# Two copies a unit earlier, and three PSUM banks for turned weights in a soft mixture of experts

## The chip, the cores and the metric

The kernel runs on one core of a Trainium2 chip. The metric is the device time of one execution in microseconds (us); the median of several executions counts. The engines are TensorE (PE: matrix products and transposes; PEld: its weight loads), VectorE (DVE), ScalarE (ACT), GpSimd (POOL) and SyncE (SP, which here only issues transfers). Each works through its own instructions in order, and they are held together by semaphores. PSUM, into which TensorE writes, has eight banks of 128 x 512 float32.

## The reference, cut to what matters

A block of three residual stages on x, 4 x 256 tokens of 256 channels: a cross attention over 4096 context rows, a causal self attention with 16 heads, and a soft mixture of 64 experts with 32 slots each. The change lies in the last one:

```python
h = layernorm(x)                                            # 1024 tokens x 256
logits = einsum('tzd,ed->tze', h, phi_w) + phi_b            # 1024 x 2048
D = softmax(logits, over the 32 slots of an expert)         # "dispatch"
C = softmax(logits, over the 64 experts of a slot)          # "combine"
X = clip(einsum('tznp,tzd->npd', D, h), -33000, 65000)      # 2048 slots x 256
X = tanh((X - mean) * rsqrt(var + 1e-5))
Y = einsum('npd,ndH->npH', X, expert_w) + expert_b          # 64 experts
y = einsum('tznp,npH->tzH', C, Y)                           # 1024 x 256
out = x + y
```

## The kernel before, in words

The 1024 tokens are 8 tiles of 128 (`TT`). The 2048 slots are cut in two ways: into 4 blocks of 512 columns for the logits (`LB`), so that there are 32 units of one tile and one block (`NU`, unit u is tile u // 4, block u % 4), and into 16 steps of 128 slots or 4 experts (`ST`) for the experts. Every engine has its own program, written out by hand as loops; the order of the work is the order of the calls in them.

*Logits stage.* For each unit, TensorE makes the logits in one of four banks (`logit`, L1774), ScalarE brings them out (`logits_out`, L1908), VectorE takes the maximum of each expert's slots (`dispatch_max`, L2007) and subtracts it straight from the bank (`dispatch_subtract`, L2012; for every fourth unit GpSimd does so from SBUF, L1724), ScalarE takes exponentials (`dispatch_exp`, L1913), VectorE sums and inverts (L2019, L2024), and GpSimd multiplies (`divide_dispatch`, L1697). TensorE starts unit u only when the bank of unit u - 4 is free (`evicted`). From unit 5 on each unit is followed by slot inputs (`early_inputs`, L1781): products of the divided dispatch weights with the normed rows `h_nat`, summed in banks 4 to 7. Beside it ScalarE takes the combine exponentials of tiles 0 to 3 by slot, four per unit from its eighth round on (`slot_exp`, L1919), from the maxima over a whole tile that VectorE takes in its rounds 4, 11, 18, 25, 28 and 31 (`combine_max`, L2028). Behind the 32 units come the remaining slot inputs (L1781, L1787).

The last two tiles of x are finished only when this stage begins. So VectorE norms tiles 6 and 7 (`norm`, L1994) in its round 2. TensorE turns the normed rows of tiles 4 to 7 behind the logits of unit 4 (`transpose_h`, L1766) into banks 6 and 7 (`PS_TURN`). In their round 5 (`v == LB + 1`) VectorE (L2051) and ScalarE (L1943) copy them to `hT`, which shows as `turned`. TensorE waits for both copies behind the logits of unit 7, since the slot inputs of slots 512 on write the same banks. Unit 16 is the first to read the copies.

*Experts stage.* VectorE clips the slot inputs and takes their statistics (`input_statistics`), GpSimd the scale, ScalarE the tanh (`input_tanh`, L1961). In step s TensorE turns the inputs of step s (`transpose_inputs`, L1805, two transposes) into bank 4 or 5, ScalarE copies them out (L1975), and TensorE multiplies the inputs of step s - 1 with their weights (`experts`, L1815, 16 instructions). VectorE adds the bias (`outputs`, L2079), ScalarE and GpSimd split the sum into a high and a low part (L1933, L1752), and `mix` adds three products of each step to the result of a tile (L1823, L1825, L1826).

For `mix` the combine weights have to be turned as well. A turn (`transpose_combine`, L1797) is four transposes into one bank, bank 0 or 1 in turns; ScalarE casts it to the high part (`combine_out`, L1929), VectorE takes the low part as bank minus high part (`combine_low`, L2085), and then the bank is free. A tile has four turns. Tiles 0 to 3 are turned in steps 4 to 7, two turns ahead of the step's experts and two behind; tiles 4 and 5 in steps 12 to 15, two turns in each; tiles 6 and 7 after the steps. ScalarE's order in a step is: tanh of the next step, copy of the turned inputs, the casts, high part of an output of two steps before. The expert weights (1 MB a step) come in through three buffers, each transfer waiting for the products of the step that used the buffer.

Of the kernel before, what the change touches and what calls it, by code (L numbers as in the profile page):

```python
# [45 lines left out]
def at_least(eng, sem, value):  # L46

    if not isinstance(value, int) or value > 0:
        eng.wait_ge(sem, value)
# [1481 lines left out]
def soft_moe(nc, x_sb, x_stats, x_mv, x_ve, x_rstd, ident, kept, disp, highs, y_hi, y_lo, expert_w, expert_b, out):  # L1531
# [18 lines left out]
    with ExitStack() as st:  # L1550
# [39 lines left out]
                   front_hi[:, 1, :]]  # L1590

        bank = kept.bank
        psL, psT, psE, psC = bank[0:4], bank[4:6], bank[6:8], bank[0:2]
        psY = [bank[2 + t // 2][:, t % 2 * HID:(t % 2 + 1) * HID] for t in range(TT // 2)] + [
            bank[t][:, 0:HID] for t in range(TT // 2, TT)]
        Y_FROM = (6, 7, 8, 9)
# [54 lines left out]
        def turned_at(s):  # L1651

            if 4 <= s < 8:
                return s - 4, 0, LB
            return (s // 2 - 2, s % 2 * 2, s % 2 * 2 + 2) if 12 <= s else None

        def mixed_until(t, s):

# [103 lines left out]
        def _(pe):  # L1762
# [29 lines left out]
            def transpose_combine(c, first, end):  # L1792
                for k in range(first, end):
                    pe.wait_ge(cmul_g, LB * c + k + 1)
                    at_least(pe, cTlo_v, LB * c + k - 1)
                    for j in range(4):
                        last = nc.tensor.transpose(psC[k % 2][:, j * P:(j + 1) * P],  # L1797
                                                   comb[:, c, (4 * k + j) * P:(4 * k + j + 1) * P], ident[:])
                    last.then_inc(cT_mm, 1)

            def transpose_inputs(s):
                pe.wait_ge(tanh_a, s + 1)
                at_least(pe, xT_a, s - 1)
                for c in range(DH):
                    last = nc.tensor.transpose(psT[s % 2][:, c * P:(c + 1) * P], xh[:, s % 2, c * P:(c + 1) * P], ident[:])  # L1805
                last.then_inc(xT_mm, 1)

            def experts(s):
# [49 lines left out]
            slot_inputs(EARLY + 4, 0, TT)  # L1858
            slot_inputs(EARLY + 5, 0, TT)
            for s in range(ST):  # L1860
                if s < 2:
                    pe.wait_ge(clip_v, 2 * s + 2)
                transpose_inputs(s)
                turn = turned_at(s)
                if s == 4:
                    pe.wait_ge(clip_v, EARLY + 4)
                if turn is not None:
                    transpose_combine(turn[0], turn[1], turn[1] + 2)
                if 1 <= s <= 2:
                    pe.wait_ge(clip_v, 2 * s + 4)  # L1870
                if s:
                    experts(s - 1)
                if s < 2:
                    slot_inputs(EARLY + 6 + s, 0, TT)
                for t in range(TT // 2):
                    first, end = mixed_until(t, s - 1), mixed_until(t, s)
                    if first == 0 and end > 0:
                        pe.wait_ge(clip_v, 14 if t < 2 else ST)
                        pe.wait_ge(cTlo_v, LB * (t + 1))
                    if end > first:  # L1880
                        mix(t, first, end)
                    if t == 0 and turn is not None and turn[2] > turn[1] + 2:
                        transpose_combine(turn[0], turn[1] + 2, turn[2])
# [19 lines left out]
        @block.scalar  # L1903
        def _(act):
            def logits_out(u):
                t, cols = unit(u)
                act.wait_ge(L_mm, u + 1)
                nc.scalar.copy(comb[:, t, cols], psL[u % 4][:]).then_inc(L_a, 1)  # L1908

            def dispatch_exp(u):  # L1910
                t, cols = unit(u)
                subtracted(act, u)
                nc.scalar.activation(disp[t][:, cols], disp[t][:, cols], ACT.Exp).then_inc(dexp_a, 1)  # L1913

            def slot_exp(i):
                c, p = i // NS, i % NS
                act.wait_ge(cneg_v, c + 1)
                column = by_slot(comb[:, c, :])[:, p, :]
                nc.scalar.activation(column, column, ACT.Exp, bias=cneg[:, c, p:p + 1],  # L1919
                                     accum_out=csum[:, c, p:p + 1]).then_inc(cslot_a, 1)  # L1920

            def combine_exp(c):
                act.wait_ge(csub_g, LB * (c - SLOTWISE + 1))
                nc.scalar.activation(comb[:, c, :], comb[:, c, :], ACT.Exp).then_inc(cexp_a, 1)

            def combine_out(c, first, end):
                for k in range(first, end):
                    act.wait_ge(cT_mm, LB * c + k + 1)
                    nc.scalar.copy(comb_hi[c][:, k * 512:(k + 1) * 512], psC[k % 2][:]).then_inc(cT_a, 1)  # L1929

            def outputs_high(s):
                act.wait_ge(mixed_v, s + 1)
                nc.scalar.copy(y_hi[:, s, :], mixed[:, s, :]).then_inc(yhi_a, 1)  # L1933

            logits_out(0)
            logits_out(1)
            slot = 0
            for v in range(NU + 1):
                if v:
                    dispatch_exp(v - 1)  # L1940
                if v == LB + 1:
                    act.wait_ge(pro_mm, 2)
                    nc.scalar.copy(hT[:, 1, HALF:2 * HALF], PS_TURN[1][:]).then_inc(pro_a, 1)  # L1943
                if v + 2 < NU:
                    logits_out(v + 2)
                if v >= FIRST_SLOTS:
                    for _ in range(PER_STEP):
                        slot_exp(slot)
                        slot += 1

            def input_tanh(s):
                q = s // 2
                if s % 2 == 0:
                    act.wait_ge(srstd_g, q + 1)
                    nc.scalar.activation(sneg[:, q, :], srstd[:, q, :], ACT.Identity, scale=-1.0).then_inc(shift_a, 1)
                    act.wait_ge(shift_a, 3 * q + 1)
                    for k in (0, 1):
                        nc.scalar.activation(snmr[:, q, k:k + 1], smv[:, q, k, 0:1], ACT.Identity, scale=sneg[:, q, k:k + 1]).then_inc(shift_a, 1)
                act.wait_ge(shift_a, 3 * q + 2 + s % 2)
                at_least(act, xT_mm, s - 1)  # L1960
                nc.scalar.activation(xh[:, s % 2, :], centred(s), ACT.Tanh, bias=snmr[:, q, s % 2:s % 2 + 1],  # L1961
                                     scale=srstd[:, q, s % 2:s % 2 + 1]).then_inc(tanh_a, 1)

            while slot < SLOTWISE * NS:
                slot_exp(slot)
                slot += 1
            combine_exp(SLOTWISE)
            combine_exp(SLOTWISE + 1)
            input_tanh(0)
            for s in range(ST):  # L1970
                if s + 1 < ST:
                    input_tanh(s + 1)
                act.wait_ge(xT_mm, s + 1)
                at_least(act, e_mm, s - 1)
                nc.scalar.copy(xhT[:, s % 2, :, :].rearrange("p c s -> p (c s)"), psT[s % 2][:, 0:DH * P]).then_inc(xT_a, 1)  # L1975
                if turned_at(s) is not None:
                    combine_out(*turned_at(s))
                if s == 2:
                    act.wait_ge(xs_mm, ST)
                if s >= 2:  # L1980
                    outputs_high(s - 2)
                if s in (8, 10):
                    combine_exp(SLOTWISE + s // 2 - 2)
            outputs_high(ST - 2)
            outputs_high(ST - 1)
            combine_out(TT - 2, 0, LB)
            act.wait_ge(ylo_g, ST)
            combine_out(TT - 1, 0, LB)

        @block.vector  # L1990
        def _(dve):
# [48 lines left out]
            for v in range(NU + 1):  # L2040
                if v < NU and not on_pool(v):
                    dispatch_subtract(v)
                if v + 1 < NU:
                    dispatch_max(v + 1)
                if v == 2:
                    dve.wait_ge(rstd_g, 2)
                    norm(TT - QT, TT)
                if v == LB + 1:
                    dve.wait_ge(pro_mm, 1)
                    dve.wait_ge(pro_v, 1)  # L2050
                    nc.vector.tensor_scalar(hT[:, 0, HALF:2 * HALF], PS_TURN[0][:], rest_rows[:], ident[:, 0:1],  # L2051
                                            ALU.mult, ALU.add).then_inc(pro_v, 1)
# [28 lines left out]
            def combine_low(c, first, end):  # L2081
                for k in range(first, end):
                    cols = slice(k * 512, (k + 1) * 512)
                    dve.wait_ge(cT_a, LB * c + k + 1)
                    nc.vector.tensor_tensor(comb_lo[:, c, cols], psC[k % 2][:], comb_hi[c][:, cols].bitcast(F32),  # L2085
                                            ALU.subtract).then_inc(cTlo_v, 1)

            combine_max(TT - 2)
# [87 lines left out]
```

## Time and profile before

| | us |
|---|---|
| median of 3 runs | 567.41 |
| the runs | 563.71, 567.92, 567.41 |
| profiled execution | 567.7 |
| its span, first to last instruction | 565.9 |
| TensorE busy | 533.9 (94%) |
| VectorE busy | 363.3 (64%) |
| ScalarE busy | 363.8 (64%) |
| GpSimd busy | 361.7 (64%) |

Mean granted TensorE clock 0.991 of full speed. The logits stage begins at 357.4 us of the span. Times of rows are counted from the start of the span. A row of a timeline gives the start, the duration, the engine, the line of the kernel, the operation, what it writes and reads, and how many instructions are merged in it; in brackets stands how long the engine was idle before, and what ended that. A merged row ends with the last instruction's end; TensorE's next instruction can start some 0.16 us before that, since its ends are modelled.

### The profile page before, as it was taken

What the parts mean: (1) busy time and instruction counts of PE and PEld (TensorE: products, weight loads), DVE (VectorE), ACT (ScalarE), POOL (GpSimd) and SP (SyncE); (2) the same over time, 40 slices, a digit from 0 to 9 for tenths busy, and PEclk for the clock granted to TensorE, in tenths of its full rate; (3) what the DMA queues carried; (4) which work ended last, traced back from release to release, by engine and by line L of the source; (5) the groups of instructions that cost most, each with busy time, mean ns of one, the idle gap of its engine ahead of it and who ended that gap; (6) DMA issues with size and microseconds to landing.
All of it is one profiled execution on the core that took longest, in us unless ns stands there. A gap on an engine that the chain in (4) does not pass through costs nothing. (4 is left out here: it accounts for less than half of the span.)

```text
span 565.9 us, 9355 instructions
## 1 busy us (share of the span) xinstructions
PE 533.9 (94%) x3256; PEld 414.5 (73%) x3256; DVE 363.3 (64%) x736; ACT 363.8 (64%) x1016; POOL 361.7 (64%) x282
## 2 busy tenths in 40 slices
PE   5898999999999999999898989889999999899998
PEld 4786888888888888777566656446555887578898
DVE  1785344564455345745776898686999998588340
ACT  2446765856584866873787886328999895666320
POOL 2775989659775784755559675243465899688500
PEclk9999999999999999999898999999999999999999
DMA  8463464675743733175139500400000643978110
GB/s 295 160 224 134 163 224 162 185 282 183 251 149 131 248 143 103 48 169 136 32 100 204 181 1 1 151 0 1 1 1 1 118 105 109 331 230 245 57 48 28
DMA packets 38669, 75.45 MB, mean 133 GB/s; under 512 B 3408, under 2 KB 27360, under 8 KB 37728
## 3 DMA queue, kind: packets, MB, share of 16 engines
q1 hardware_dynamic: 36864, 68.57, 39.6%
q10 hardware_dynamic: 1760, 6.30, 3.1%
q8 instruction: 26, 0.43, 0.3%
q14 instruction: 19, 0.16, 0.1%
HBM read 68.56 MB, written 6.30 MB: 132 GB/s over the span
## 5 line engine op out<-in xcount | busy, mean ns | idle before, releaser
L387 POOL TENSOR_TENSOR ctxT_lo<-front,ctxT_hi 128x1024 fp32r<-128x1024 f32 x32 | 76.9, 2408 | 46.2 <-ACT ctxT_hi L682 46.2
L503 PE MATMUL ps<-ctx_both,pT_hi 128*128 128x512 f32 x256 | 94.6, 409 | 1.9 <-DVE pT_lo L858 1.9
L392 POOL TENSOR_TENSOR ctx_both<-ctx_in,ctx_both 128x1024 fp32r<-128x1024 f32 x32 | 76.5, 2395 | 16.3 <-ACT ctx_both L687 16.3
L505 PE MATMUL ps<-ctx_both,pT_lo 128*128 128x256 f32 x256 | 71.9, 281 | 0.0
L1774 PE MATMUL ps<-front,turned 128*128 128x512 f32 x128 | 61.0, 605 | 0.3 <-PEq L1008 0.3
L850 DVE TENSOR_SCALAR_CACHE_REDUCE first<-ps,qbk 128x512 f32<-128x512 f32 x32 | 24.0, 750 | 55.5 <-PE ps L475 53.2
L706 ACT CAST pT_hi<-ps 128x512 fp32r<-128x512 f32 x64 | 34.0, 590 | 38.3 <-PE ps L487 38.3
L503 PEld LDWEIGHTS ps<-ctx_both,pT_hi 128*128 128x128 f32 x256 | 48.2, 188 | 13.1 <-DVE pT_lo L858 2.8
L858 DVE TENSOR_TENSOR pT_lo<-ps,pT_hi 128x512 fp32r<-128x512 f32 x64 | 41.1, 685 | 16.4 <-ACT pT_hi L706 16.4
L1919 ACT ACTIVATE comb<-comb,cneg 128x64 f32<-128x64 f32 x128 | 50.8, 411 | 0.0
L505 PEld LDWEIGHTS ps<-ctx_both,pT_lo 128*128 128x128 f32 x256 | 48.5, 190 | 0.1
L475 PE MATMUL ps<-ctxT_hi,qk_hi 128*128 128x512 f32 x128 | 41.1, 402 | 2.6 <-DVE qk_lo L842 2.2
L1710 POOL TENSOR_TENSOR comb<-comb,cinv 128x512 f32<-128x512 f32 x32 | 40.6, 1285 | 0.8 <-DVE cinv L2037 0.8
L475 PE MATMUL ps<-ctxT_hi,qk_lo 128*128 128x512 f32 x128 | 40.0, 394 | 0.0
L475 PE MATMUL ps<-ctxT_lo,qk_hi 128*128 128x512 f32 x128 | 39.7, 391 | 0.0
L682 ACT CAST ctxT_hi<-front 128x1024 fp32r<-128x1024 f32 x32 | 33.7, 1057 | 8.1 <-PE ps L475 3.8
L1774 PEld LDWEIGHTS ps<-front,turned 128*128 128x128 f32 x128 | 24.4, 193 | 19.7 <-issue 18.2
L1697 POOL TENSOR_TENSOR more<-more,dinv 128x512 f32<-128x512 f32 x24 | 25.1, 1048 | 19.6 <-DVE dinv L2024 19.6
L1409 DVE TENSOR_REDUCE nmax<-ps 128x2 f32<-128x512 f32 (+1 forms) x48 | 31.6, 671 | 7.9 <-PE ps L1210 6.9
L1826 PE MATMUL ps<-y_hi,comb_lo 128*128 128x256 f32 x128 | 36.1, 282 | 0.0
L1105 POOL TENSOR_TENSOR eB<-eB,rinv 128x1024 f32<-128x1024 f32 x16 | 30.3, 1893 | 8.9 <-DVE rinv L1417 8.9
L1351 ACT ACTIVATE eB<-ps,nmax 128x256 f32<-128x256 f32 x64 | 29.8, 483 | 8.9 <-DVE nmax L1409 8.9
(260 smaller groups left out, 1436.1 us busy)
## 6 DMA issues: line engine op xcount, KB each, us to landing
front<-in_ctx_turned_dram SPq DMA_DIRECT2D x32, 512.0 KB, 4.7
ctx_in<-in_ctx_dram SPq DMA_DIRECT2D x32, 512.0 KB, 3.5
back<-in_L_ffn_expert_w_dram SPq DMA_DIRECT2D x11, 1024.0 KB, 5.9
turned<-in_L_ffn_expert_w_dram SPq DMA_DIRECT2D x5, 1024.0 KB, 5.8
phi_piece<-in_phi_turned_dram ACTq DMA_DIRECT2D x8, 512.0 KB, 6.3
phi_less_dram<-phi_piece ACTq DMA_DIRECT2D x4, 512.0 KB, 3.1
front<-phi_less_dram SPq DMA_DIRECT2D x1, 2048.0 KB, 14.0
front<-in_L_ffn_expert_b_dram SPq DMA_DIRECT2D x4, 512.0 KB, 10.2
```

The source lines that it names most:

```text
L387: nc.gpsimd.tensor_tensor(ctxT_lo[:, n % RING, :, :], turned_in[:, n % SLOTS, :, :], ctxT_hi[:, n % RING, :, :].bitcast(F32), ALU.subtract ...
L392: nc.gpsimd.tensor_tensor(ctx_both[:, m % RING, :, 1, :], by_tile(m), ctx_both[:, m % RING, :, 0, :].bitcast(F32), ALU.subtract).then_inc( ...
L475: last = nc.tensor.matmul(pS[q][:], a[:, dh, q * P:(q + 1) * P], k[:, n % RING, dh, :], start=step == 0, stop=step == 5)
L503: nc.tensor.matmul(pO[q][:], pT_hi[:, c % 2, q, cols], ctx_both[:, m % RING, j, :, :].rearrange("p k d -> p (k d)"), start=c == 0 and j == ...
L505: last = nc.tensor.matmul(pO[q][:, 0:D], pT_lo[:, c % 2, q, cols], ctx_both[:, m % RING, j, 0, :], start=False, stop=c == NCH - 1 and j == ...
L682: nc.scalar.copy(ctxT_hi[:, n % RING, :, :], turned_in[:, n % SLOTS, :, :]).then_inc(ctxThi_a, 1)
L706: nc.scalar.copy(pT_hi[:, c % 2, q, :], probs_banks(c)[q][:]).then_inc(probsThi_a, 1)
L858: nc.vector.tensor_tensor(pT_lo[:, c % 2, q, :], probs_banks(c)[q][:], pT_hi[:, c % 2, q, :].bitcast(F32), ALU.subtract).then_inc(probsTlo ...
L1710: nc.gpsimd.tensor_tensor(part, part, cinv[:, c, :].unsqueeze(1).broadcast_to([P, EB, NS]), ALU.mult).then_inc(cmul_g, 1)
L1774: last = nc.tensor.matmul(psL[u % 4][:], hT[:, c, t * P:(t + 1) * P], phiT[:, c, cols], start=c == 0, stop=c == DH - 1)
L1826: last = nc.tensor.matmul(psY[t], comb_lo[:, t, cols], y_hi[:, s, :], start=False, stop=s == ST - 1, skip_group_check=True)
L1919: nc.scalar.activation(column, column, ACT.Exp, bias=cneg[:, c, p:p + 1], accum_out=csum[:, c, p:p + 1]).then_inc(cslot_a, 1)
```

## The change

The kernel does the same arithmetic. In the logits stage VectorE norms tiles 6 and 7 in its round 1 instead of 2, and VectorE and ScalarE copy the turned rows in round 4 instead of 5 (on VectorE ahead of that round's sum and of the tile maximum, on ScalarE ahead of bringing out unit 6). In the experts stage the turned inputs always go to bank 4, and the turned weights of tiles 0 to 5 go round banks 0, 1 and 5; those of tiles 6 and 7 keep banks 0 and 1. The waits follow: a turn waits for the low part three turns back instead of two, and the inputs' transposes of step s for the copy of step s - 1 instead of s - 2.

```diff
                    front_hi[:, 1, :]]
 
         bank = kept.bank
-        psL, psT, psE, psC = bank[0:4], bank[4:6], bank[6:8], bank[0:2]
+        psL, psT, psE, psC = bank[0:4], bank[4], bank[6:8], (bank[0], bank[1], bank[5])
         psY = [bank[2 + t // 2][:, t % 2 * HID:(t % 2 + 1) * HID] for t in range(TT // 2)] + [
             bank[t][:, 0:HID] for t in range(TT // 2, TT)]
         Y_FROM = (6, 7, 8, 9)
@@ -1653,6 +1653,10 @@
             if 4 <= s < 8:
                 return s - 4, 0, LB
             return (s // 2 - 2, s % 2 * 2, s % 2 * 2 + 2) if 12 <= s else None
+
+        def turn_bank(c, k):
+
+            return psC[(LB * c + k) % 3 if c < TT - 2 else k % 2]
 
         def mixed_until(t, s):
 
@@ -1792,17 +1796,17 @@
             def transpose_combine(c, first, end):
                 for k in range(first, end):
                     pe.wait_ge(cmul_g, LB * c + k + 1)
-                    at_least(pe, cTlo_v, LB * c + k - 1)
+                    at_least(pe, cTlo_v, LB * c + k - (2 if c < TT - 2 else 1))
                     for j in range(4):
-                        last = nc.tensor.transpose(psC[k % 2][:, j * P:(j + 1) * P],
+                        last = nc.tensor.transpose(turn_bank(c, k)[:, j * P:(j + 1) * P],
                                                    comb[:, c, (4 * k + j) * P:(4 * k + j + 1) * P], ident[:])
                     last.then_inc(cT_mm, 1)
 
             def transpose_inputs(s):
                 pe.wait_ge(tanh_a, s + 1)
-                at_least(pe, xT_a, s - 1)
+                at_least(pe, xT_a, s)
                 for c in range(DH):
-                    last = nc.tensor.transpose(psT[s % 2][:, c * P:(c + 1) * P], xh[:, s % 2, c * P:(c + 1) * P], ident[:])
+                    last = nc.tensor.transpose(psT[:, c * P:(c + 1) * P], xh[:, s % 2, c * P:(c + 1) * P], ident[:])
                 last.then_inc(xT_mm, 1)
 
             def experts(s):
@@ -1858,8 +1862,8 @@
             slot_inputs(EARLY + 4, 0, TT)
             slot_inputs(EARLY + 5, 0, TT)
             for s in range(ST):
-                if s < 2:
-                    pe.wait_ge(clip_v, 2 * s + 2)
+                if s == 0:
+                    pe.wait_ge(clip_v, 2)
                 transpose_inputs(s)
                 turn = turned_at(s)
                 if s == 4:
@@ -1926,7 +1930,7 @@
             def combine_out(c, first, end):
                 for k in range(first, end):
                     act.wait_ge(cT_mm, LB * c + k + 1)
-                    nc.scalar.copy(comb_hi[c][:, k * 512:(k + 1) * 512], psC[k % 2][:]).then_inc(cT_a, 1)
+                    nc.scalar.copy(comb_hi[c][:, k * 512:(k + 1) * 512], turn_bank(c, k)[:]).then_inc(cT_a, 1)
 
             def outputs_high(s):
                 act.wait_ge(mixed_v, s + 1)
@@ -1938,7 +1942,7 @@
             for v in range(NU + 1):
                 if v:
                     dispatch_exp(v - 1)
-                if v == LB + 1:
+                if v == LB:
                     act.wait_ge(pro_mm, 2)
                     nc.scalar.copy(hT[:, 1, HALF:2 * HALF], PS_TURN[1][:]).then_inc(pro_a, 1)
                 if v + 2 < NU:
@@ -1972,7 +1976,7 @@
                     input_tanh(s + 1)
                 act.wait_ge(xT_mm, s + 1)
                 at_least(act, e_mm, s - 1)
-                nc.scalar.copy(xhT[:, s % 2, :, :].rearrange("p c s -> p (c s)"), psT[s % 2][:, 0:DH * P]).then_inc(xT_a, 1)
+                nc.scalar.copy(xhT[:, s % 2, :, :].rearrange("p c s -> p (c s)"), psT[:, 0:DH * P]).then_inc(xT_a, 1)
                 if turned_at(s) is not None:
                     combine_out(*turned_at(s))
                 if s == 2:
@@ -2042,10 +2046,10 @@
                     dispatch_subtract(v)
                 if v + 1 < NU:
                     dispatch_max(v + 1)
-                if v == 2:
+                if v == 1:
                     dve.wait_ge(rstd_g, 2)
                     norm(TT - QT, TT)
-                if v == LB + 1:
+                if v == LB:
                     dve.wait_ge(pro_mm, 1)
                     dve.wait_ge(pro_v, 1)
                     nc.vector.tensor_scalar(hT[:, 0, HALF:2 * HALF], PS_TURN[0][:], rest_rows[:], ident[:, 0:1],
@@ -2082,7 +2086,7 @@
                 for k in range(first, end):
                     cols = slice(k * 512, (k + 1) * 512)
                     dve.wait_ge(cT_a, LB * c + k + 1)
-                    nc.vector.tensor_tensor(comb_lo[:, c, cols], psC[k % 2][:], comb_hi[c][:, cols].bitcast(F32),
+                    nc.vector.tensor_tensor(comb_lo[:, c, cols], turn_bank(c, k)[:], comb_hi[c][:, cols].bitcast(F32),
                                             ALU.subtract).then_inc(cTlo_v, 1)
 
             combine_max(TT - 2)
```

## Rows read from the trace of the kernel before

**Rows 1.** Busy time by stretch: stretch, its length, engines' busy us, clock, DMA share, GB/s.

```profile
383.00:440.00 57.00, 57.00 (x179) 33.60 (x178) 50.25 (x82) 54.08 (x211) 30.74 (x29) 1.00 0.00 1
440.00:480.00 40.00, 40.00 (x222) 32.69 (x221) 38.40 (x82) 31.67 (x120) 36.19 (x35) 1.00 0.49 109
480.00:500.00 20.00, 17.28 (x167) 12.39 (x169) 12.55 (x23) 13.99 (x34) 13.05 (x15) 1.00 0.92 288
500.00:566.00 66.00, 62.40 (x579) 55.26 (x571) 32.96 (x41) 23.42 (x51) 29.57 (x28) 1.00 0.37 119
```

**Rows 2.** Timeline of TensorE, start of the logits stage.

```profile
357.41 8.82 PE L1774 MATMUL ps<-front,turned 128*128 128x512 f32 x20 [0.32 <-PEq L1008]
...
367.58 1.09 PE L1766 MATMUL ps<-ident,wide 128*128 128x128 f32 x8 [1.35 <-DVE wide L1994]
368.51 1.88 PE L1774 MATMUL ps<-front,turned 128*128 128x512 f32 x4
...
373.67 1.88 PE L1774 MATMUL ps<-front,turned 128*128 128x512 f32 x4
378.11 1.13 PE L1781 MATMUL ps<-wide,first 128*128 128x256 f32 x4 [2.55 <-DVE turned L2051]
379.07 3.29 PE L1774 MATMUL ps<-front,turned 128*128 128x512 f32 x4
...
383.35 1.88 PE L1774 MATMUL ps<-front,turned 128*128 128x512 f32 x4
```

**Rows 3.** One microsecond of the same table by stretches.

```profile
381.00:382.00 1.00, 1.00 (x2) 0.34 (x1) 0.00 (x0) 0.00 (x0) 1.00 (x2) 0.50 0.00 0
```

**Rows 4.** Timeline of VectorE, the same stretch.

```profile
363.45 0.69 DVE L2007 TENSOR_REDUCE dmax<-comb 128x16 f32<-128x512 f32 x1 [0.30 <-ACT comb L1908]
...
366.07 1.46 DVE L1994 TENSOR_SCALAR wide<-x_sb,x_mv,x_rstd 128x256 f32<-128x256 f32 x2
...
372.53 3.61 DVE L2028 TENSOR_REDUCE cneg<-comb 128x32 f32<-128x2048 f32 x1
376.05 0.69 DVE L2012 TENSOR_TENSOR first<-ps,dmax 128x512 f32<-128x512 f32 x1
...
377.24 0.81 DVE L2051 TENSOR_SCALAR turned<-ps,rest_rows,ident 128x512 f32<-128x512 f32 x1
```

**Rows 5.** Timeline of GpSimd, the same stretch.

```profile
366.23 1.15 POOL L1724 TENSOR_TENSOR first<-comb,dmax 128x512 f32<-128x512 f32 x1
...
379.01 1.05 POOL L1697 TENSOR_TENSOR first<-first,dinv 128x512 f32<-128x512 f32 x1 [5.27 <-DVE dinv L2024]
```

**Rows 6.** Waits from 480 to 500 us: total us, times, longest.

```profile
PE ps L1797 <- DVE comb_lo L2085: 2.7, 4, 0.8
```

**Rows 7.** The table by stretches, 376 to 396 us.

```profile
376.00:396.00 20.00, 17.89 (x51) 10.51 (x52) 13.57 (x27) 12.65 (x45) 8.34 (x8) 0.91 0.00 1
```

**Rows 8.** Timeline of TensorE in the experts stage.

```profile
479.11 0.44 PE L1805 MATMUL ps<-ident,xh 128*128 128x128 f32 x2
479.39 1.04 PE L1797 MATMUL ps<-ident,comb 128*128 128x128 f32 x8
...
481.48 1.23 PE L1797 MATMUL ps<-ident,comb 128*128 128x128 f32 x8
...
483.60 1.23 PE L1797 MATMUL ps<-ident,comb 128*128 128x128 f32 x8 [0.67 <-DVE comb_lo L2085]
...
522.75 1.22 PE L1797 MATMUL ps<-ident,comb 128*128 128x128 f32 x8
```

**Rows 9.** Timeline of ScalarE in the experts stage.

```profile
478.50 0.35 ACT L1975 COPY xhT<-ps 128x256 f32<-128x256 f32 x1
...
482.14 1.19 ACT L1929 CAST first_hi<-ps 128x512 fp32r<-128x512 f32 x2 [1.05 <-PE ps L1797]
...
484.90 1.06 ACT L1929 CAST first_hi<-ps 128x512 fp32r<-128x512 f32 x2
```

**Rows 10.** Timeline of VectorE in the experts stage.

```profile
485.52 1.29 DVE L2085 TENSOR_TENSOR comb_lo<-ps,first_hi 128x512 fp32r<-128x512 f32 x2 [1.46 <-ACT first_hi L1929]
```

## The prediction

> **What bounds the kernel now.** I read the table by stretches first. From 383 to 480 us TensorE is busy for the whole of both stretches, while VectorE has 50.25 and ScalarE 54.08 of the first 57 us: there TensorE sets the pace, with ScalarE close behind. From 480 to 500 it is busy for 17.28 of 20 us, so something else ends steps there; after 500 it has 62.40 of 66 [rows 1]. What is shifted ahead of 383 us arrives at the end if the others can follow; what is saved between 480 and 500 arrives too.
>
> Then TensorE's timeline at the start of the logits stage. Twenty matmul instructions (units 0 to 4, four each, 0.43 us apart) start at 357.41, so unit 5 could follow at 366.01. The eight transposes of the last tiles' normed rows start at 367.58, released by VectorE's norm. Units 5 and 7 start at 368.51 and 373.67: 2.58 us per unit (1.72 for the logits, 0.86 for the slot inputs that follow). Unit 7's logits leave TensorE free at 373.67 + 1.72 = 375.39, but the slot inputs start at 378.11, released by VectorE's copy of the turned rows. The logits of unit 8 then take 3.29 us instead of 1.88, and unit 9 starts only at 383.35 [rows 2]. The reader is to see three losses in one place. The third is the clock: the granted clock was 0.50 (the 1.2 GHz level) at 381 us, after TensorE had stood still from 375.4 to 378.1, and 1.00 (2.4 GHz) from 383 on [rows 1, 3].
>
> VectorE's timeline says why. The norm runs at 366.07, after the third unit's work. The copy of the turned rows runs at 377.24, behind a 3.61 us maximum over a whole tile (372.53) and behind the next unit's subtraction (376.05) [rows 4]. Its input was there since the transposes ended, near 368.7.
>
> **Part one, the logits.** Nothing is added or removed; two norms and two copies go one unit earlier on their engines.
>
> *The norm.* It would follow the maximum at 363.45, so from 364.05. It took 1.46 us where it stood, while GpSimd ran an operation of 1.15 us from 366.23 [rows 4, 5]; I let it take as long at 364. It is done by 365.5 and TensorE no longer waits at 366.01. Gain: 367.58 - 366.01 = 1.57, and no less than the 1.35 that the trace marks as idle; I take 1.5. Behind the norm on VectorE stand sum and reciprocal of unit 0 and the subtraction of unit 2, which with it move back by its length, to an end near 366.9. Unit 6's logits overwrite that bank; they start near 369.5 (366.0 for the transposes, 0.93 for these, 2.58 for unit 5). This cover is 2.6 us; if it were gone, unit 6 would be late by the difference. Ahead of 369.7 us VectorE has done the same work in both orders.
>
> *The copies.* Unit 5's logits end near 368.7, ScalarE brings them out by 369.4, VectorE takes their maximum by 370.9 and then copies the turned rows: 0.81 us, done near 371.7 [rows 4]. ScalarE's copy goes ahead of bringing out unit 6, which is not there before 371: cost nothing, cover over 0.5 us. TensorE wants both copies after unit 7's logits, near 373.9, so the wait falls away whole: 378.11 - 375.39 = 2.72. The maximum over a tile comes 0.8 us later in its queue at most, ending at 376.1 as before; the subtraction of unit 5 ends by 376.7. TensorE wants its bank back for unit 9 near 377.3. That wait is late next, with 0.6 us to spare. After it comes GpSimd's division of unit 4, which started at 379.01 on VectorE's reciprocal [rows 5]. With the copy out of the way it starts near 378.2 and ends near 379.2, while TensorE asks for it at 379.0: between 0 and 0.3 us are paid. I take 0.1.
>
> *The clock.* From 378.11 to 383.35 TensorE did 3.44 us of work (0.86 + 1.72 + 0.86) in 5.24: 1.80 us lost [rows 2]. Without the two pauses it should not fall there. A gain of 0 to 1.8; I take 1.8, since between 480 and 500, with four marked pauses of 2.7 us in all, the longest 0.8, the granted clock stayed at 1.00 [rows 1, 6].
>
> Sum: 1.5 + 2.7 - 0.1 + 1.8 = 5.9.
>
> *Can the others follow?* The tile maximum that ends at 376.1 does not move, so VectorE must make up 5.9 us behind it. From 376 to 396 it was busy 13.57 of 20 us [rows 7]; that is 6.4 us idle, and 0.8 of copy is gone from there: 7.2 against 5.9. ScalarE was idle for more (12.65 busy). From 396 on every engine is in the state it was in, 5.9 us earlier, and TensorE stays the pace.
>
> **Part two, the experts.** Turn n (four transposes of a weight tile) needed VectorE's low part of turn n - 2, and now of turn n - 3, for tiles 0 to 5. The round trip: cast at 482.14, next turn at 483.60 after 0.67 us of waiting; 1.46 us from cast to release [rows 8, 9]. In steps 4 to 7 the marked pauses are 2.7 us [rows 6], and a group of eight transposes takes 1.23 us where its second turn waits, 1.04 where it does not [rows 8], which happens six times: 1.1 more. So 3.8 us can be had. Not all goes. ScalarE casts turns 2 and 3 from 482.14, and then has y_hi, the scale and shift, a tanh and the copy of the turned inputs before its next cast at 484.90; that one's low part starts at 485.52 [rows 9, 10]. Turn 7 now needs this low part (turn 4's), which ends near 486.2, while TensorE would be ready at 485.4. Going through the sixteen turns so, waits remain at turn 5 (0.5), 7 (0.8), 13 (0.4), 15 (0.3): 2.0. Gain 1.8. The group of eight at 522.75 (1.22 us) gives some 0.2 more [rows 8]. Sum 2.0; between 0 and 3.8.
>
> *The added wait.* The inputs' transposes of step s now wait for ScalarE's copy of step s - 1. Behind them on TensorE stand the turns and the experts' products, and through these VectorE's outputs. The tightest place is step 4: copy 478.50 to 478.85, transposes at 479.11 [rows 8, 9]; 0.26 us to spare. In the later steps the products and sums of a step of 4 to 5 us lie between. Cost nothing; if the cover at step 4 is gone, some tenths once. The dropped wait of step 1 was for work long done.
>
> The Trainium skill speaks against part two: its page "TensorE: Matmul & The Clock Gate", section "HAM oscillation — how this bites in real kernels", tells of a kernel in which "Adding PSUM double-buffering gave no further gain". By that the second part is worth 0 and the sum 5.9. No run here shows it yet; in the rows, VectorE's release of a bank ends the pauses.
>
> **Sum.** 5.9 + 2.0 = 7.9 us. The profiled execution took 567.7 us around its span of 565.9, the median of the runs is 567.4; 567.4 - 7.9 = 559.5.
>
> **The rivals.**
> *A, the forecast:* 559.5. Chance 0.56. Its own bounds: the gain lies between 5.4 + 0.5 and 6.1 + 3.8, so 557.5 to 561.5.
> *B, the third bank gives nothing,* because the chain cast, low part, turn stays as it is, or because the weight transfers bind (DMA share 0.92 from 480 to 500 [rows 1]): gain 5.9, time 561.5. Against it: the pauses end with VectorE's low part, not with a transfer. 0.16.
> *C, the clock falls all the same* in the logits' first units: 7.9 - 1.8 = 6.1, time 561.3. For it: TensorE's rate fell a microsecond after the pause had ended, so it may be decided by what lies before. 0.12.
> *D, VectorE becomes the bound after unit 8:* 7.2 us of slack is an average, and it may lie in the wrong places; then some 3 of the 5.9 are given back and the time is 562.5. 0.08.
> *E, slower:* with the experts' stage 6 us earlier and its pauses reshaped, the granted clock falls between 480 and 500. TensorE's work there is 17.28 us at full rate [rows 1]; each microsecond of it at half rate costs another. From 7.9 us of work at half rate on, the change loses; with all of it, 9.4 us are lost and the time is 576.8. Against it: 1.00 in that stretch, though it has the most pauses. 0.04. The same page of the Trainium skill, section "A second HAM failure mode: psum-queue depth-cycling", has a kernel that cycles through PSUM banks and whose clock goes up and down for it; here the trace shows the cycling (480 to 500) without the fall.
> The remaining 0.04: more than forecast, or a difference between executions.
>
> **How the numbers follow.** A measurement of this kernel tells about 1% (5.7 us) from no change, so faster means below 561.7. A lies there whole (0.56), B and C just inside with some two thirds of their chance (0.18), and 0.02 of the rest: 0.76. Slower: E, and a little for what I don't see, 0.05. Within 1%: 0.19. The range goes from A's lower bound, 557.5, to D's 562.5, with 0.8 added on both sides since one of the three runs lay 3.7 below the median: 556.7 to 563.3. Outside it are E and the odd differences, under 0.1 together, and of the rest what I have judged too narrowly.
>
> **What would show it.** Right: transposes at about 366.0 without a pause before them; no pause after unit 7; clock 1.00 from 366 to 386; unit 9 near 377.4; the last slot inputs ending 5.9 us earlier than before; TensorE's pauses before the turns between 475 and 495 down from 2.7 to below 2. Wrong: a new pause before unit 9 or 10 (released by VectorE or GpSimd), a pause before the inputs' transposes released by ScalarE's copy, VectorE without idle time after 390, or a granted clock below 1.00 at either place.

## The result and the profile after

The changed kernel took 558.21 us as the median of 4 runs (557.25 to 562.01), the kernel before 565.83 (563.71 to 567.92, now 4 runs). The ratio is 0.9858, with a 95% interval from 0.981 to 0.9906. A second series of the same kernel, in the experiments below, gave 0.9841 (0.9802 to 0.988). The forecast was 559.5, with a range from 556.7 to 563.3.

The head of the profile after, its line of busy times and the row of TensorE's granted clock in 40 slices:

```profile
span 556.0 us, 9354 instructions
...
PE 529.2 (95%) x3256; PEld 413.1 (74%) x3256; DVE 362.0 (65%) x736; ACT 363.4 (65%) x1016; POOL 361.6 (65%) x282
...
PEclk9999999999999999999899999999999999999999
```

The span is 556.0 us, 9.9 less than before, but not all of that is the change. The logits stage begins at 356.18 us instead of 357.41, and nothing ahead of it was touched. So every length below is counted from that stage's first matmul instruction: to the end it is 565.9 - 357.41 = 208.5 us before, and 556.0 - 356.18 = 199.8 after. The change is worth 8.7 us in these two profiles.

TensorE's timeline after, to be read against [rows 2] (times from the start of the span, duration, instruction, how many are merged, in brackets the idle time before):

```profile
356.18 8.82 PE L1778 MATMUL ps<-front,turned 128*128 128x512 f32 x20 [0.32 <-PEq L1008]
364.84 1.04 PE L1770 MATMUL ps<-ident,wide 128*128 128x128 f32 x8
365.71 1.88 PE L1778 MATMUL ps<-front,turned 128*128 128x512 f32 x4
367.43 1.03 PE L1785 MATMUL ps<-wide,first 128*128 128x256 f32 x4
368.29 1.88 PE L1778 MATMUL ps<-front,turned 128*128 128x512 f32 x4
370.01 1.03 PE L1785 MATMUL ps<-wide,first 128*128 128x256 f32 x4
370.87 1.88 PE L1778 MATMUL ps<-front,turned 128*128 128x512 f32 x4
372.59 1.03 PE L1785 MATMUL ps<-wide,first 128*128 128x256 f32 x4
373.45 1.88 PE L1778 MATMUL ps<-front,turned 128*128 128x512 f32 x4
...
376.03 1.88 PE L1778 MATMUL ps<-front,turned 128*128 128x512 f32 x4
```

The rows left out are of the same two kinds and have no bracket either. The reader is to see that none but the first has one. The transposes follow the twentieth logits instruction, the slot inputs at 372.59 follow unit 7, and unit 9 starts 376.03 - 356.18 = 19.85 us into the stage; before, it was 383.35 - 357.41 = 25.94 [rows 2]. That is 6.1 us.

VectorE's timeline after, for [rows 4]:

```profile
362.82 0.73 DVE L1998 TENSOR_SCALAR wide<-x_sb,x_mv,x_rstd 128x256 f32<-128x256 f32 x2
...
368.92 0.80 DVE L2055 TENSOR_SCALAR turned<-ps,rest_rows,ident 128x512 f32<-128x512 f32 x1
...
370.52 3.63 DVE L2032 TENSOR_REDUCE cneg<-comb 128x32 f32<-128x2048 f32 x1
374.08 0.68 DVE L2016 TENSOR_TENSOR first<-ps,dmax 128x512 f32<-128x512 f32 x1
```

The norm takes 0.73 us here instead of 1.46. The copy of the turned rows stands ahead of the tile maximum (370.52). The subtraction behind that is over at 374.76, and unit 9 wants its bank at 376.03.

The table by stretches after, for [rows 1, 3, 7], with the clock as the third number from the right, and TensorE's waits for the low part from 455 to 500 us, for [rows 6]:

```profile
374.00:382.00 8.00, 8.00 (x26) 4.63 (x25) 7.86 (x17) 5.85 (x19) 4.40 (x5) 1.00 0.00 0
382.00:386.00 4.00, 4.00 (x14) 2.36 (x13) 3.08 (x7) 4.00 (x16) 2.43 (x3) 1.00 0.00 0
```

```profile
PE ps L1801 <- DVE comb_lo L2089: 1.4, 4, 0.4
```

TensorE is busy for the whole of 374 to 386 us at full clock. In the experts stage 1.4 us of marked waits are left of 2.7. The turns' timeline after, for [rows 8]:

```profile
473.98 1.09 PE L1801 MATMUL ps<-ident,comb 128*128 128x128 f32 x8
...
476.13 0.63 PE L1801 MATMUL ps<-ident,comb 128*128 128x128 f32 x4 [0.40 <-DVE comb_lo L2089]
...
478.77 0.63 PE L1801 MATMUL ps<-ident,comb 128*128 128x128 f32 x4 [0.40 <-DVE comb_lo L2089]
...
480.29 0.63 PE L1801 MATMUL ps<-ident,comb 128*128 128x128 f32 x4 [0.24 <-DVE comb_lo L2089]
...
485.50 0.63 PE L1801 MATMUL ps<-ident,comb 128*128 128x128 f32 x4 [0.40 <-DVE comb_lo L2089]
```

These are turns 5, 7, 9 and 13, counted from 0. What stands in the way of turn 7 at 478.77 is the cast and low part of turn 4, which come behind a tanh (476.57) and a copy (477.06) on ScalarE. ScalarE and VectorE after:

```profile
477.06 0.35 ACT L1979 COPY xhT<-ps 128x256 f32<-128x256 f32 x1
477.32 1.67 ACT L1933 CAST first_hi<-ps 128x512 fp32r<-128x512 f32 x3
```

```profile
477.93 1.29 DVE L2089 TENSOR_TENSOR comb_lo<-ps,first_hi 128x512 fp32r<-128x512 f32 x2 [1.35 <-ACT first_hi L1933]
```

For the length of steps 0 to 7, the inputs' first and ninth transposes before:

```profile
467.80 0.41 PE L1805 MATMUL ps<-ident,xh 128*128 128x128 f32 x2
...
499.39 0.38 PE L1805 MATMUL ps<-ident,xh 128*128 128x128 f32 x2
```

and after:

```profile
460.41 0.41 PE L1809 MATMUL ps<-ident,xh 128*128 128x128 f32 x2
...
490.04 0.38 PE L1809 MATMUL ps<-ident,xh 128*128 128x128 f32 x2
```

31.59 us became 29.63. From the stage's first instruction to the first of these it was 110.39 us and is now 104.23. Behind the second it was 66.5 us to the end and is 66.0. So the 8.7 us are 6.2 + 2.0 + 0.5.

### The profile page after: what moved, and what is told of

Read it like the earlier page. It is cut to its first block and busy times, and to the rows that moved or that the text cites. A ratio compares the mean times of both kernels' runs of the same rounds, so it can differ in the third digit from the quotient of the medians.

```text
span 556.0 us, 9354 instructions
## 1 busy us (share of the span) xinstructions
PE 529.2 (95%) x3256; PEld 413.1 (74%) x3256; DVE 362.0 (65%) x736; ACT 363.4 (65%) x1016; POOL 361.6 (65%) x282
## 5 line engine op out<-in xcount | busy, mean ns | idle before, releaser
L1778 PE MATMUL ps<-front,turned 128*128 128x512 f32 x128 | 59.6, 593 | 0.3 <-PEq L1008 0.3
L850 DVE TENSOR_SCALAR_CACHE_REDUCE back<-ps,qbk 128x512 f32<-128x512 f32 x32 | 24.0, 751 | 16.5 <-PE ps L475 16.5
```

What stands on the lines that cost most here:

```text
L850: nc.vector.tensor_scalar(scores[q][:, c * CH:(c + 1) * CH], pS[q][:], qbk[:, b * QT + q:b * QT + q + 1], None, ALU.add, ALU.max, accum_ou ...
L1778: last = nc.tensor.matmul(psL[u % 4][:], hT[:, c, t * P:(t + 1) * P], phiT[:, c, cols], start=c == 0, stop=c == DH - 1)
```

## The experiments

Each kernel ran in 3 or 5 rounds beside the kernel before on the same chip, where an interval is given. The executions of one kernel lie up to 7 us apart, so the lengths from the stage's first matmul instruction are the sharper measure. All of them, in us; the first two columns are "to the first inputs' transposes" and "from these to the ninth":

| kernel | logits | steps 0 to 7 | to the end | ratio (95%) |
|---|---|---|---|---|
| before | 110.4 | 31.6 | 208.5 | |
| before, second profile | 108.7 | 31.6 | 206.8 | |
| after | 104.2 | 29.6 | 199.8 | 0.9858 (0.981 to 0.9906) |
| after, second profile | 104.3 | 29.6 | 200.0 | 0.9841 (0.9802 to 0.988) |
| logits part only | 104.3 | 31.6 | 202.3 | 0.9899 (0.9863 to 0.9934) |
| experts part only | 110.4 | 29.6 | 206.1 | 0.9947 (0.9919 to 0.9976) |
| norm only | 107.2 | 31.6 | 205.3 | 0.9946 (0.9923 to 0.9968) |
| norm only, second profile | 107.3 | 31.6 | 205.3 | |
| copies only | 105.8 | 31.6 | 203.9 | 0.9935 (0.9907 to 0.9962) |
| one bank for inputs | 110.4 | 31.6 | 208.5 | 1.0018 (0.999 to 1.0047) |
| unit 8 ahead | 107.0 | 31.6 | 205.1 | 0.9946 (0.9921 to 0.9971) |
| one long pause | 110.7 | 31.6 | 208.8 | 1.0028 (0.9996 to 1.006) |
| four banks | 104.3 | 27.9 | 198.2 | 0.9834 (0.9797 to 0.9872) |
| four banks, second series | 104.3 | 27.9 | 198.3 | 0.983 (0.9791 to 0.9868) |

**The two parts alone.** The logits part is the diff's last three `v ==` conditions on the kernel before; the experts part is the rest.

> Only the logits part: norm and both copies one unit earlier, experts as before. My theory (both pauses and the clock's fall go, nothing is given back): 6.0 us less than before, ratio 0.989; the inputs' first transposes 104.2 us after the stage's first matmul instead of 110.4. Rival (the gain is swallowed by VectorE later): under 4 us, with new pauses of TensorE between 380 and 460 us.

> Only the experts part: one bank for the turned inputs, three for the turned weights of tiles 0 to 5. My theory: 2.0 to 2.5 us less than before (ratio 0.996), and the waits of the turns from 480 to 500 us go from 2.7 to about 1.5 us. Rival B (a further bank gives nothing because the chain cast, low part, turn stays): under 0.5 us. The logits stage with its pause of 2.55 us and its fall of the clock is as before.

Measured: 6.2 us less to the end with the logits part (561.29 us, median of 6 runs, beside 567.76 of 29), and 2.4 with the experts part (564.75, 12 runs). The parts add up: 6.2 + 2.4 = 8.6 against 8.7. With the logits part alone TensorE has no new pause between unit 9 and the first inputs' transposes; VectorE took nothing of the gain back. With the experts part alone the marked waits of the turns from 480 to 500 us are 1.4 us, as expected. From the logits stage to the end they fall from 3.0 us in the kernel before to 1.8. Before:

```profile
PE ps L1797 <- DVE comb_lo L2085: 3.0, 5, 0.8
```

and with the experts part alone, where the waits for the copy and for the norm are still there:

```profile
PE ps L1785 <- DVE turned L2055: 2.6, 1, 2.6
PE ps L1801 <- DVE comb_lo L2089: 1.8, 5, 0.4
PE ps L1770 <- DVE wide L1998: 1.4, 1, 1.4
```

**Norm alone, copies alone.** The first pair of lines is the one run; the second pair, on VectorE and on ScalarE, is the other.

```diff
-                if v == 2:
+                if v == 1:
                     dve.wait_ge(rstd_g, 2)
...
-                if v == LB + 1:
+                if v == LB:
```

> Only the norm one unit earlier, both copies in their old place. My theory: the transposes come 1.6 us earlier, VectorE no longer waits for unit 5 and so the copy comes about 1.5 us earlier too; the pause after unit 7 stays near 2.6 us, with a fall of the clock behind it. 1.5 us less than before. Rival: the copy stays where it was because it hangs on the tile maximum alone; then the pause grows to 4.2 us and the gain is 0.

> Only the two copies one unit earlier, the norm in its old place. My theory: the pause of 1.35 us before the transposes stays, the one after unit 7 goes (2.7 us), and the clock doesn't fall (1.8 us): 4.5 us less than before, ratio 0.992. Rival C (the fall comes from the first pause, or from the place, and not from the pause after unit 7): the granted clock still reads 0.50 for some 3 us near 380, and the gain is 2.7 us.

The copies alone came out as expected: 4.6 us less in the profiles (563.73 us, 12 runs), with the pause of 1.35 us kept and a clock of 1.00 behind it. The norm alone did not: 3.2 us less instead of 1.5 (564.21 us, 12 runs; the ratio's upper end, 0.9968, leaves out 1.5 us). TensorE's timeline with the norm alone, and one stretch of its table:

```profile
377.69 1.13 PE L1781 MATMUL ps<-wide,first 128*128 128x256 f32 x4 [2.61 <-DVE turned L2051]
378.66 1.88 PE L1774 MATMUL ps<-front,turned 128*128 128x512 f32 x4
```

```profile
374.00:382.00 8.00, 5.39 (x17) 2.96 (x16) 7.27 (x12) 2.46 (x5) 3.10 (x3) 1.00 0.00 0
```

The pause is there as expected (2.61 us), but the logits of unit 8 behind it take 1.88 us, not 3.29: the clock stayed at 1.00. Some 1.5 us are the order of the work, the other 1.7 are the clock, which had fallen in the profile that this one is compared with.

**Filling the pause.** The kernel before, with unit 8's logits issued ahead of the wait for the copies:

```diff
-                logit(u)
+                if u != LB + 4:
+                    logit(u)
...
                 if u == LB + 3:
+                    logit(u + 1)
                     pe.wait_ge(pro_v, 2)
```

> The kernel before with the logits of unit 8 issued ahead of the wait for the two copies, all else in place: 1.7 us of the pause of 2.7 us are filled with the same work, and some 1.0 us of pause is left. Theory: the clock fell because TensorE stood still before unit 8, so it stays at 1.00 now: 1.7 + 1.8 = 3.5 us less than before. Rival: the clock falls at this place whatever the length of the pause; 1.7 us less, and 0.50 in the table near 380.

```profile
371.76 3.60 PE L1774 MATMUL ps<-front,turned 128*128 128x512 f32 x8
376.23 1.99 PE L1781 MATMUL ps<-wide,first 128*128 128x256 f32 x8 [0.87 <-DVE turned L2053]
378.06 1.88 PE L1774 MATMUL ps<-front,turned 128*128 128x512 f32 x4
```

0.87 us of pause are left, the clock did not fall, and the stage is 3.4 us shorter with every norm and copy in its old place (3.5 were expected). Beside a profile of the kernel before in which the clock did not fall either (206.8, below), it is 1.7 us shorter: that much is the filled pause.

**Is the fall of the clock steady?** Three runs were made for this. The long pause is the norm-only kernel with both copies in round `LB + 2`.

> The norm one unit earlier, and both copies one unit LATER than in the kernel before: one pause of some 4.6 us after unit 7, where the kernel before has two of 1.4 and 2.6 us with three units between them. What is open is why the clock fell behind the two pauses, but not behind the one of 2.6 us in the run with the norm alone. Theory 1 (it is how much TensorE stands still there in all, here 4.6 us against 4.0): the granted clock reads 0.50 for some 3 us behind the pause, and the time is 0.5 to 1 us above the kernel before. Theory 2 (it takes the first pause): 1.00 throughout, some 1 us below the kernel before.

> The norm one unit earlier alone, a second look at its clock. If the missing fall behind the one pause of 2.6 us belongs to this order of the work, the granted clock is 1.00 again from 366 to 386 us, and unit 9 starts 22.7 us after the stage's first matmul instruction. If it was chance, it reads 0.50 this time and unit 9 comes at 24.5.

> The kernel before, a further look at its clock: 0.50 behind the two pauses, as in the three profiles that have both (the kernel before, experts part only, one bank for the inputs); unit 9 starts 25.9 us after the stage's first matmul instruction. Another number there would say that the fall is not steady.

The kernel before, second profile:

```profile
377.06 1.13 PE L1781 MATMUL ps<-wide,first 128*128 128x256 f32 x4 [2.56 <-DVE turned L2051]
378.02 1.88 PE L1774 MATMUL ps<-front,turned 128*128 128x512 f32 x4
...
380.61 1.88 PE L1774 MATMUL ps<-front,turned 128*128 128x512 f32 x4
```

```profile
374.00:382.00 8.00, 5.44 (x18) 3.06 (x17) 7.23 (x13) 2.33 (x4) 3.10 (x3) 1.00 0.00 0
```

The one long pause:

```profile
381.66 2.07 PE L1781 MATMUL ps<-wide,first 128*128 128x256 f32 x4 [4.63 <-DVE turned L2051]
383.53 2.51 PE L1774 MATMUL ps<-front,turned 128*128 128x512 f32 x4
```

```profile
374.00:382.00 8.00, 3.37 (x11) 1.72 (x10) 7.96 (x10) 2.80 (x5) 3.13 (x3) 0.96 0.00 0
382.00:386.00 4.00, 4.00 (x9) 2.35 (x9) 0.45 (x2) 0.00 (x0) 1.06 (x2) 0.65 0.00 0
```

The norm-only kernel kept its clock again (205.3 us to the end, as in its first profile, though its total of this one run is 567.37 us). The kernel before this time had both pauses (1.35 and 2.56 us) and a clock of 1.00 throughout: unit 9 started 24.26 us into the stage (380.61 - 356.35), not 25.94. So its fall is not steady. With the two pauses, 3.9 us in all, the clock fell in three profiles of four (the kernel before once of twice, experts part only, one bank for inputs); with one of 4.6 us in the only one; with 2.6 us in none of two; with less or none at all in none of the other seven. The fall behind one long pause speaks against theory 2 and for theory 1, the amount of standing still. The time of the long pause went less clearly: 208.8 us to the end against 208.5, ratio 1.0028, where theory 1 had 0.5 to 1 us more. The price of one fall is shown by one and the same kernel: 25.94 - 24.26 = 1.7 us.

Theory 1 can't be the whole, since the kernel before had the same two pauses in both profiles. The mean granted clock is on record for nearly all executions, not only for the profiled ones, and says more. In each of the fourteen profiles a fall takes 0.003 off the mean of the execution: none gives 1.000, one 0.997, two 0.994 and three 0.991. The profiles show falls at two places only, from 270 to 320 us (none, one or two) and here.

| pauses at the start of the logits stage | executions | 1.000 | 0.997 | 0.994 or 0.993 | 0.991 |
|---|---|---|---|---|---|
| both (before, experts part only, one bank for inputs) | 93 | 14 | 0 | 54 | 25 |
| one of 4.6 us | 10 | 0 | 0 | 6 | 4 |
| one of 2.6 us (norm only) | 12 | 0 | 9 | 2 | 1 |
| 2.2 us or less in all (the others) | 52 | 7 | 35 | 10 | 0 |

With both pauses no execution reads 0.997, that is exactly one fall; with less, that is the usual number. So the fall here seems to come in 79 of the 93 executions, always together with one in the stage ahead, and to stay away in the 14 that have none there. The profiles agree: the three with a fall here have one ahead of it, the one without has none. That both go together is counted, not explained; no run varied it. The rows of the long pause and of the norm alone support theory 1 with 10 and 12 executions instead of one and two profiles, but they too count falls without showing their place.

**The added wait alone.** `psT` is one bank, `psC` keeps two:

```diff
-                at_least(pe, xT_a, s - 1)
+                at_least(pe, xT_a, s)
```

> The kernel before with one bank for the turned inputs and still two for the turned weights: the added wait alone. My theory: no change, 0 to 0.3 us more than before; no pause of TensorE before the inputs' transposes that ScalarE's copy ends. Rival (the added wait costs, and the third bank pays for it): 0.5 us more or above, with such pauses.

208.5 us to the end as before, 31.6 us for steps 0 to 7, and none of TensorE's marked waits is one for ScalarE's copy. The wait shows no cost, and the interval of the ratio holds 1.

**A fourth bank.** On the changed kernel:

```diff
-        psL, psT, psE, psC = bank[0:4], bank[4], bank[6:8], (bank[0], bank[1], bank[5])
+        psL, psT, psE, psC = bank[0:4], bank[4], bank[6:8], (bank[0], bank[1], bank[5], bank[3])
...
-            return psC[(LB * c + k) % 3 if c < TT - 2 else k % 2]
+            return psC[k % 4 if c < TT // 2 else (LB * c + k) % 3 if c < TT - 2 else k % 2]
...
-                    at_least(pe, cTlo_v, LB * c + k - (2 if c < TT - 2 else 1))
+                    at_least(pe, cTlo_v, LB * c + k - (3 if c < TT // 2 else 2 if c < TT - 2 else 1))
+                    if c == 0 and k == 3:
+                        pe.wait_ge(clip_v, ST)
```

> The changed kernel with a fourth bank (bank 3, free until the third tile's sums begin) for the turned weights of tiles 0 to 3; a turn then waits for the low part four turns back. Theory: the 1.4 us that the turns of steps 5 to 7 still wait go; ScalarE, with casts, tanh and copies, becomes the pace of these steps, so some of it comes back as pauses before the inputs' transposes: 0.5 to 1.3 us less than the changed kernel, some 8.5 to 9.5 less than the kernel before. Rival: ScalarE is the pace already, then nothing (0 to 0.2 us).

> The changed kernel once more, beside the fourth bank and on the same chip: 7.5 to 8.5 us less than before, the sum of the two parts if they add up (6.0 and 2.2).

> The fourth bank once more, since its first run's times can't be told from the changed kernel's, while its trace is 1.6 us shorter from the stage's first matmul instruction to the end. Expected from the trace: 198.2 us from there to the end again, and 9 to 10.5 us less than the kernel before (8.7 for the changed kernel).

```profile
PE ps L1803 <- DVE comb_lo L2091: 0.3, 1, 0.3
```

Steps 0 to 7 take 27.9 us instead of 29.6 in both profiles, and the whole is 1.6 us shorter from the stage's start (198.2 and 198.3 against 199.8 and 200.0). The marked waits of the turns up to 500 us fall from 1.4 to 0.3. That is more than the 0.5 to 1.3 us expected, and no pause before the inputs' transposes came back for it. The changed kernel itself is 8.5 us shorter than the kernel before from the stage's start (208.5 - 200.0), as expected; its median in that series is 10.0 us lower. The total times don't show the fourth bank: 558.14 and 557.75 us beside 558.21 and 557.84 for the changed kernel, and against the kernel before its second series has 8.7 us less, short of the 9 to 10.5 expected. The two intervals nearly cover each other. By the traces it is the better kernel; by the total times that is open.

## Why the prediction was right

*The pauses of the logits stage.* Forecast 1.5 + 2.7 - 0.1, without the clock. The transposes came 1.5 us earlier (364.84 - 356.18 = 8.66 against 10.17 us into the stage), unit 7's pause went whole, and nothing was paid behind it. In the kernel before without a fall, unit 9 came at 24.26 us; after, at 19.85. That is 4.4 us where 4.1 was the forecast. The term that was off is the norm's length: I let it take 1.46 us at its new place as well, and it took 0.73. So everything behind it on VectorE came 0.7 us sooner, the subtraction of unit 5 had 1.3 us to spare instead of 0.6, and GpSimd's division was over at 377.36, ahead of the slot inputs at 377.75, so the 0.1 was not paid. The rest of the difference is some 0.1 us that each of the first instructions behind a pause took longer (1.09 and 1.13 us before, 1.04 and 1.03 after).

*The two terms by themselves* were right for the copies (2.7 us, and 2.8 measured with no fall on either side: 203.93 us to the end against 206.75), and for the norm (1.5 us; 205.3 against 206.75, so 1.45).

*The clock.* The size, 1.8 us, was right for the profile that I had (1.7 between two profiles of one kernel), and rival C, a fall all the same, was not seen: 1.00 in both profiles of the changed kernel. What was wrong is the tacit step from one profile to the median: the fall is not in every execution. By the mean clocks it is in 60 of the 69 executions of the kernel before in the experiments' series, so by an estimate from these the median holds some 1.5 of the 1.7 us. The reason that I gave, that four pauses of 2.7 us in all between 480 and 500 don't bring it down, showed no more than that those short pauses left it alone.

*VectorE can follow.* Right. The logits part brought the inputs' first transposes forward by 6.2 us, as much as unit 9 (6.1).

*The experts.* Forecast 1.8 in steps 4 to 7 and 0.2 behind them; measured 2.0 and 0.5. I had placed waits at turns 5, 7, 13 and 15 with 0.5, 0.8, 0.4 and 0.3 us. They came at 5, 7, 9 and 13 with 0.40, 0.40, 0.24 and 0.40. The mechanism at turn 7 was right: it waits for turn 4's low part, which starts at 477.93, 0.6 us behind a cast that stands behind tanh and copy. So I had left 2.0 us of waits where 1.4 are marked. The 0.5 behind the steps is the group of eight at 522.75: I counted only its own 0.18 us (1.22 against 1.04) and overlooked that it started 0.52 us behind the inputs' transposes (522.23 to 522.75), where it now starts 0.22 behind them (512.88 to 513.10). The trace marks no wait in that gap. Before, ahead of that group [rows 8], and after:

```profile
522.23 0.38 PE L1805 MATMUL ps<-ident,xh 128*128 128x128 f32 x2
```

```profile
512.88 0.38 PE L1809 MATMUL ps<-ident,xh 128*128 128x128 f32 x2
513.10 1.04 PE L1801 MATMUL ps<-ident,comb 128*128 128x128 f32 x8
```

*The added wait* cost nothing, as forecast, and the run with it alone shows that. *Rival B* did not come true, and the quoted sentence of the Trainium skill ("TensorE: Matmul & The Clock Gate", section "HAM oscillation — how this bites in real kernels") does not carry over to this kernel: here the rotation over three banks is worth 2.4 us and a fourth bank another 1.6 by the traces. The pauses that VectorE's release of a bank ended are what shrank. *Rival D* falls with the logits part alone. *Rival E* was not seen: the granted clock stayed at 1.00 between 470 and 500 us in all fourteen profiles.

*The number.* 559.5 was forecast from the then median of three runs, 567.4. The 7.9 us of the forecast compare with 8.7 between the two profiles and with 7.0 where the kernel before has no fall (206.8 - 199.8). That the measured median came within 1.3 us of 559.5 is in part luck: the median of the kernel before moved from 567.4 to 565.8 with one more run, and the stages ahead alone differ by up to 5 us between profiles.

## What to carry to other kernels

Look at the order of an engine's queue before its load: VectorE was 64% busy, and TensorE waited for a 0.8 us copy behind a 3.6 us reduction that nobody needed yet. For a ring of buffers between three engines, count the round trip from write to release and the turns that fit in it; here the third buffer and, by the traces, the fourth paid, though ScalarE had a tanh and a copy between its casts. And measure a change from the first instruction of the stage that it touches, when the stages ahead differ from one execution to the next.

## What the runs showed of the hardware that was not expected

The logits stage began between 355.5 and 360.5 us in the fourteen profiles, with the same instructions ahead of it. The largest part arises at the start of the program. The same eight matmuls in the kernel before and in the four-bank kernel:

```profile
13.53 1.97 PE L456 MATMUL ps<-h1T,phib 128*128 128x256 f32 x8 [0.34 <-DVE small L946]
```

```profile
15.81 3.49 PE L456 MATMUL ps<-h1T,phib 128*128 128x256 f32 x8 [0.34 <-DVE small L946]
```

They start 2.3 us apart and take 1.97 and 3.49 us, and the products behind them start 3.8 us apart (16.58 and 20.38). The granted clock reads 1.00 from 13 to 20 us in both profiles, so it does not show this. The Trainium skill, page "TensorE: Matmul & The Clock Gate", section "Part 1: The HAM clock gate (the "warmup" mystery)", says that how long a program's first matmuls run slow varies from run to run; the durations of these rows agree. Another place is the second stage, from 260 to 320 us, with a mean granted clock of 0.94 in the kernel before and of 1.00 in its second profile:

```profile
260.00:320.00 60.00, 53.99 (x405) 38.78 (x406) 44.41 (x98) 43.79 (x181) 38.96 (x49) 0.94 0.61 147
```

```profile
260.00:320.00 60.00, 52.37 (x419) 38.11 (x420) 45.73 (x100) 44.47 (x186) 40.57 (x51) 1.00 0.61 147
```

What a fall costs depends on where it lies. Five profiles have one between 300 and 320 us (the kernel before, logits part only, experts part only, the first of the norm alone, the second of four banks), and these take 66.0 to 66.1 us from the first matmul of L1241 (284.32 us in the kernel before) to the first of L1258 (350.38). The other nine take 64.4 to 64.9, though seven of them have a fall between 270 and 290. A third place has nothing to do with the granted clock, which reads 1.00 there: between 215 and 235 us three profiles take 0.4 to 0.7 us longer than the rest, and why is open.

The second thing is the norm: the same two VectorE operations took 1.46 us while GpSimd was running a tensor operation, and 0.73 where GpSimd stood idle (its rows: 366.23 before [rows 5]; after, its next operation starts at 364.51). It is 1.46 in all six profiles with the norm at its old place and 0.73 in all eight with it at the new one. That the one caused the other was not tested by itself.
